# A mixture-of-experts stage in seven steps: every piece one step later, two sets of output banks, token buffers refilled after the combination, pads at the front of the buckets

## The reference, cut to what matters

```python
x = x + gnn(layernorm(x), adj, ...)               # two layers: softmax(h h^T) * adj, three projections, layernorm, relu
xt = layernorm(x).reshape(-1, 384)
route_prob = softmax((xt @ enc_w + enc_b) @ sw_w + sw_b)
expert = argmax(route_prob)                       # one of 8 for each token
h = gelu(xt @ w1[expert] + b1[expert])            # 384 -> 64
out = (h @ w2[expert] + b2[expert]) * max(route_prob)
x = x + out
```

## Time and profile before

| | |
|---|---|
| median of the runs | 2221.36 us |
| profiled execution | 2229.13 us |
| its span, first to last instruction | 2227.4 us |
| mean granted TensorE clock | 0.986 |
| TensorE (PE) busy | 95% |
| VectorE (DVE) busy | 75% |
| ScalarE (ACT) busy | 67% |
| GpSimd (POOL) busy | 63% |
| DMA queue of SP | 99.6 MB, 15.1% of 16 engines |
| DMA queue of GpSimd | 50.6 MB, 6.0% of 16 engines |

### The profile page before, as it was taken

One profiled execution on the slowest core, in us unless ns is written; L12 is line 12 of the kernel. 1 busy time (PEld: TensorE's weight loads), 2 busy tenths in 40 slices (PEclk: granted clock), 3 DMA queues, 4 the chain that ended last, 5 costly groups with the idle time before them and its releaser, 6 DMA issues. The chain is left out here.

```text
span 2227.4 us, 56587 instructions
## 1 busy us (share of the span) xinstructions
PE 2116.7 (95%) x13576; PEld 2035.7 (91%) x13577; DVE 1661.4 (75%) x5442; ACT 1496.4 (67%) x3901; POOL 1405.0 (63%) x3274
## 2 busy tenths in 40 slices
PE   6999999999999999999999999999999999578886
PEld 5999999999999999999999998999999999456665
DVE  4777777777777777777777776777777777657775
ACT  4777777677676776677777766776777766356664
POOL 2556666666666666666666666666666666535555
PEclk9999999999999999999999999999999999789998
DMA  7101111111111111111111111111111111256664
GB/s 188 31 26 49 49 37 49 49 45 49 41 45 49 49 45 50 42 49 49 49 43 47 49 49 42 45 49 49 46 48 41 45 49 33 105 184 208 221 224 144
DMA packets 94261, 153.77 MB, mean 69 GB/s; under 512 B 17627, under 2 KB 70700, under 8 KB 93954
## 3 DMA queue, kind: packets, MB, share of 16 engines
q1 hardware_dynamic: 75844, 99.61, 15.1%
q0 software_dynamic: 17408, 50.62, 6.0%
q10 hardware_dynamic: 704, 0.10, 0.0%
HBM read 96.11 MB, written 57.32 MB: 69 GB/s over the span
## 5 line engine op out<-in xcount | busy, mean ns | idle before, releaser
L421 PE MATMUL bank<-wT_hi,hT_hi 128*128 128x384 f32 x2304 | 797.9, 346 | 11.4 <-issue 5.4
L423 PE MATMUL bank<-wT_hi,hT_lo 128*128 128x384 f32 x2304 | 774.5, 336 | 0.0
L422 PE MATMUL bank<-wT_lo,hT_hi 128*128 128x384 f32 x2304 | 773.0, 336 | 0.0
L421 PEld LDWEIGHTS bank<-wT_hi,hT_hi 128*128 128x128 f32 x2304 | 434.9, 189 | 19.2 <-ACT bank L614 11.1
L422 PEld LDWEIGHTS bank<-wT_lo,hT_hi 128*128 128x128 f32 x2304 | 435.0, 189 | 0.0
L423 PEld LDWEIGHTS bank<-wT_hi,hT_lo 128*128 128x128 f32 x2304 | 433.8, 188 | 0.0
L1145 POOL TENSOR_TENSOR hT_lo<-hT,hT_hi 128x384 fp32r<-128x384 f32 x256 | 263.5, 1029 | 23.9 <-ACT hT_hi L679 22.4
L674 ACT ACTIVATE hT<-bank 128x384 f32<-128x384 f32 x256 | 126.1, 493 | 202.5 <-PE bank L413 180.9
L650 ACT CAST right_hi<-bank 128x384 fp32r<-128x384 f32 x256 | 123.0, 480 | 180.1 <-PE bank L423 179.2
L1548 POOL DMA_INDIRECT out_dram<-out_rows,tok x144 | 144.1, 1000 | 136.4 <-DVE out_rows L1519 100.7
L1200 POOL TENSOR_SCALAR_AFFINE_SELECT deltaT_hi<-turned_hi 128x128 fp32r<-128x128 f32 x256 | 87.7, 343 | 216.0 <-ACT turned_hi L656 208.5
(11 more groups left out here) (183 smaller groups left out, 5142.9 us busy)
## 6 DMA issues: line engine op xcount, KB each, us to landing
tok<-buckets SPq DMA_DIRECT2D x72, 388.0 KB
x_in<-in_x_dram SPq DMA_DIRECT2D x128, 192.0 KB, 2.5
x_res<-in_x_dram SPq DMA_DIRECT2D x128, 192.0 KB, 2.4
adj_in<-in_adj_dram SPq DMA_DIRECT2D x128, 64.0 KB, 2.4
buckets<-pads SPq DMA_DIRECT2D x9, 388.0 KB
out_dram<-out_rows,tok POOLq DMA_INDIRECT x144
buckets<-rows,dest_words POOLq DMA_INDIRECT x128, 2.8
w_top<-in_L_ffn_w_dram SPq DMA_DIRECT2D x2, 768.0 KB
```

Source lines behind the costliest of these rows:

```text
L421: pe.matmul(o, hi, w_hi, start=False, stop=False, skip_group_check=True)
L422: pe.matmul(o, hi, w_lo, start=False, stop=False, skip_group_check=True)
L423: last = pe.matmul(o, lo, w_hi, start=False, stop=(c == C - 1), skip_group_check=True)
```

## The change

1. **Pads at the front.** Every expert's rows now begin FRONT = 256 rows after e x CAP, and the pads fill the 256 rows ahead of them. Their place is known at compile time, and SP stores all nine pad tiles in step 26 of the graph stage (PAD_STEP = FIRST - 1). The last tile of an expert is no longer its rows and pads behind them: it is the last 256 rows before the expert's end, so that it repeats rows of the tile ahead of it, or takes in front pads.
2. **Tile table by partitions.** `tile_table` works on 72 partitions, one for each tile, with small operations; the number of tiles of an expert comes by rounding with 2^23 in place of a comparison with 64 limits. Two transposes on TensorE turn rows and experts back to one partition; a matmul and two more operations make `again`, a table that adds 32768 to the token number of every repeated row, so that the scatter leaves it out.
3. **Refill.** `load(j)` waits for `y_ready` of tile j-8 (combined) and for `ids_kept` in place of the landing of its scatter. The token numbers are therefore copied out of `tok`, with `again` added, by a new GpSimd operation `keep_ids` into `row_ids`, in step j+2, ahead of the scatters of tile j-4.
4. **Seven steps.** Copies in step j+2 (before j+1), `hidden` j+3 (j+2), gelu j+4 (j+2), `output` j+5 (j+4), `combine` and `store` j+6 (j+5). ScalarE does its gelu first in a step. `output` has two sets of two banks and waits for tile j-2; `hidden` moves into the free halves of the transposes' second banks, which adds one wait for gelu each to `turn` and `copy_last`.

The diff, cut to its core:

```diff
-    TILES_OF = TOKENS // TILE
+    FRONT, ROUNDER = TILE, float(1 << 23)
...
+                        if isinstance(i, int) and i == PAD_STEP:
+                            sp.wait_ge(pads_made, 1)
+                            for row in [e * CAP for e in range(E)] + [TAIL]:
+                                sp.dma_start(buckets[row:row + TILE, :].rearrange("(p t) w -> p t w", t=T), pads[:]
+                                             ).then_inc(pads_stored, 16)
...
                     steps(sp, first_steps)
-                    sp.wait_ge(pads_made, 1)
-                    sp.dma_start(buckets[TAIL:TAIL + TILE, :].rearrange("(p t) w -> p t w", t=T), pads[:]
-                                 ).then_inc(pads_stored, 16)
-                    sp.wait_ge(ends_ready, 1)
-                    for e in range(E):
-                        row = sp.value_load(end_words[0:1, e:e + 1], min_val=e * CAP, max_val=e * CAP + TOKENS)
-                        sp.dma_start(buckets[bass.ds(row, TILE), :].rearrange("(p t) w -> p t w", t=T), pads[:]
-                                     ).then_inc(pads_stored, 16)
...
+                    pe.wait_ge(table_done, 2)
+                    pe.transpose(rows_of, per_tile["row"][0:TILES, :], ident[0:TILES, 0:TILES])
+                    pe.transpose(experts_of, per_tile["expert_at_most"][0:TILES, :], ident[0:TILES, 0:TILES]
+                                 ).then_inc(table_turned, 1)
+                    pe.wait_ge(table_done, 3)
+                    pe.matmul(twice_of, per_tile["twice_wide"][0:TILES, :], ident[0:TILES, 0:TILES], start=True, stop=True
+                              ).then_inc(table_turned, 1)
...
                         dve.wait_ge(ends_done, 1)
-                        dve.tensor_copy(end_words[:], ends_of[0:1, :]).then_inc(ends_ready, 1)
                         dve.wait_ge(route_consts_made, 1)
-                        dve.tensor_tensor(o["held"][:], ends_of[0:1, :], o["bases"][:], ALU.subtract).then_inc(table, 1)
+                        dve.tensor_tensor(o["held"], ends_of[0:TILES, :], o["bases"], ALU.subtract).then_inc(table, 1)
...
-                        dve.tensor_tensor(o["filled_tiles"][:], o["starts"][:],
-                                          o["held"][:].unsqueeze(2).broadcast_to([1, E, TILES_OF]), ALU.is_lt
+                        dve.tensor_scalar(o["rough"], o["held"], 1.0 / TILE, (TILE - 1) / 2.0 / TILE, ALU.mult, ALU.add
-                        dve.tensor_reduce(o["tiles_of"][:], o["filled_tiles"][:], AX_X, ALU.add).then_inc(table, 1)
...
+                        dve.tensor_scalar(o["rounded"], o["rough"], ROUNDER, None, ALU.add).then_inc(table, 1)
+                        dve.wait_ge(table, 4)
+                        dve.tensor_scalar(o["tiles_of"], o["rounded"], ROUNDER, None, ALU.subtract).then_inc(table, 1)
+                        dve.tensor_tensor(o["lower_tiles"], o["lower"],
+                                          o["tiles_of"].unsqueeze(1).broadcast_to([TILES, E, E]), ALU.mult
+                        dve.tensor_reduce(o["tiles_upto"], o["lower_tiles"], AX_X, ALU.add).then_inc(table, 1)
+                        dve.tensor_scalar(o["behind"], o["tiles_upto"], o["number"][:, 0:1], None, ALU.is_le
...
-                        dve.tensor_tensor(o["behind"][:], o["numbers"][:],
-                                          o["tiles_upto"][:].unsqueeze(1).broadcast_to([1, TILES, E]), ALU.is_ge
-                        dve.tensor_reduce(o["expert"][:], o["behind"][:], AX_X, ALU.add).then_inc(table, 1)
-                        dve.tensor_tensor(o["skipped"][:], o["behind"][:],
-                                          o["skip"][:].unsqueeze(1).broadcast_to([1, TILES, E]), ALU.mult
+                        dve.tensor_reduce(o["expert"], o["behind"], AX_X, ALU.add).then_inc(table, 1)
+                        dve.tensor_tensor_reduce(o["skipped"], o["behind"], o["tiles_of"], 1.0, 0.0, ALU.mult, ALU.add,
+                                                 o["skip"]).then_inc(table, 1)
...
+                        dve.scalar_tensor_tensor(o["own_end"], o["experts"], o["expert"][:, 0:1], o["ends"],
+                                                 ALU.is_equal, ALU.mult).then_inc(table, 1)
+                        dve.scalar_tensor_tensor(o["in_expert"], o["skip"], -float(TILE), o["straight"],
+                                                 ALU.mult, ALU.add).then_inc(table, 1)
+                        dve.tensor_reduce(o["end"], o["own_end"], AX_X, ALU.add).then_inc(table, 1)
+                        dve.scalar_tensor_tensor(o["in_buckets"], o["expert"], float(CAP), o["in_expert"],
                                                  ALU.mult, ALU.add).then_inc(table, 1)
-                        dve.tensor_scalar(tile_row[:], o["row"][:], float(TAIL), None, ALU.min).then_inc(tiles_ready, 1)
+                        dve.tensor_scalar(o["row"], o["end"], -float(TILE), o["in_buckets"][:, 0:1], ALU.add, ALU.min
+                                          ).then_inc(table_done, 1)
+                        dve.wait_ge(table_done, 2)
+                        dve.tensor_tensor(o["twice"], o["in_buckets"], o["row"], ALU.subtract).then_inc(table, 1)
+                        dve.wait_ge(table_turned, 1)
+                        dve.tensor_copy(tile_row[:], rows_of).then_inc(tiles_ready, 1)
+                        dve.tensor_copy(tile_expert[:], experts_of).then_inc(tiles_ready, 1)
+                        dve.wait_ge(table, 15)
+                        dve.tensor_scalar(o["twice_wide"], ones[0:TILES, :], o["twice"][:, 0:1], None, ALU.mult
+                                          ).then_inc(table_done, 1)
+                        dve.wait_ge(table_turned, 2)
+                        for t in range(T):
+                            dve.tensor_scalar(again[:, :, t], twice_of, per_tile["position"][:, t:t + 1], float(2 * TOKENS),
+                                              ALU.is_gt, ALU.mult).then_inc(tiles_ready, 1)
...
-                            dve.memset(counts[1][:, BATCH, e:e + 1], float(e * (CAP // P))).then_inc(filled, 1)
+                            dve.memset(counts[1][:, BATCH, e:e + 1], float((e * CAP + FRONT) // P)).then_inc(filled, 1)
...
-            hidden_banks = (bank[4], bank[5])
-            y_banks = (bank[6], bank[7])
-
-            OUTPUT, GELUS, DEPTH = 4, 4, 5
+            FREE_HALF = slice(TILE, 2 * TILE)
+            hidden_banks = (bank[1][:, FREE_HALF], bank[3][:, FREE_HALF])
+            y_banks = ((bank[4], bank[5]), (bank[6], bank[7]))
+
+            COPIES, HIDDEN, GELU, OUTPUT, DEPTH = 2, 3, 4, 5, 6
+            GELUS = 4
...
                         if past(j, RING):
-                            sp.wait_ge(stored[k % OUT_RING], 16 * T // OUT_RING * (j - RING - k % OUT_RING) + 16 * T)
+                            sp.wait_ge(y_ready, T * (j - RING) + T)
+                            sp.nop(nofuse=True)
+                            sp.wait_ge(ids_kept, j - RING + 1)
                         row = sp.value_load(tile_row[0:1, j:j + 1] if isinstance(j, int) else
                                             tile_row[0:1, bass.ds(j, 1)], min_val=0, max_val=TAIL)
...
+                        if past(j, 4):
+                            pe.wait_ge(gelu_ready, j - 3)
...
-                        o = hidden_banks[k % 2][:, 0:TILE]
+                        o = hidden_banks[k % 2]
...
-                            if past(j, 1):
-                                pe.wait_ge(y_ready, T * (j - 1) + t + 1)
-                            o, rows = y_banks[t][:, 0:D], slice(t * P, (t + 1) * P)
+                            if past(j, 2):
+                                pe.wait_ge(y_ready, T * (j - 2) + t + 1)
+                            o, rows = y_banks[k % 2][t][:, 0:D], slice(t * P, (t + 1) * P)
...
                     def step(i, k):
                         if there(i - 1):
                             turn(i - 1, k - 1)
-                        if there(i - 2):
-                            hidden(i - 2, k - 2)
+                        if there(i - HIDDEN):
+                            hidden(i - HIDDEN, (k - HIDDEN) % RING)
                         if there(i - OUTPUT):
                             output(i - OUTPUT, (k - OUTPUT) % RING)
...
                     def step(i, k):
+                        if there(i - GELU):
+                            gelu(i - GELU, (k - GELU) % RING)
                         if there(i):
                             normalise(i, k)
-                        if there(i - 1):
-                            pick_w1(i - 1, k - 1)
-                            copy_first(i - 1, k - 1)
-                        if there(i - 2):
-                            gelu(i - 2, k - 2)
-
-                    act.wait_ge(tiles_ready, 1)
+                        if there(i - COPIES):
+                            copy_first(i - COPIES, (k - COPIES) % RING)
+                            pick_w1(i - COPIES, (k - COPIES) % RING)
...
@@ -1497,6 +1535,7 @@
```

(29 more changed lines are left out.)

81 lines of the change are left out of this document (43 added, 38 removed).

## The result

The changed kernel takes 2167.91 us at the median of four runs (2166.76 to 2170.39), the kernel before, beside it, 2221.69 (2217.87 to 2224.03): a ratio of 0.976, with a 95% interval from 0.9748 to 0.9772. 2186.1 us was predicted, in a range from 2156 to 2212. The gain is 54 us, not 35. The profiled execution took 2170.39 us, its span is 2168.4. (The profiled execution of before lay 7.8 us above its median; so the spans differ by 59.0 us, the medians by 54.)

A forecast was written before the change was run, and what follows sets the result against it. A ring of load latencies was taken to bound the expert stage. First scatter 1966.3, plus scatters 185.8, kept numbers 36.7 and landing 3.3 gave 2192.1, 35.3 under the old span; from 2221.4 that gives 2186.1 us, range 2156 to 2212.

The forecast's parts named there:

- rival A: Expert stage: GpSimd paces, at 3.0 to 3.25 us a tile, 2177 to 2195 us; chance 0.43.
- B: Expert stage: TensorE paces, kept numbers cost 0.2 us or less, 2.66 to 2.85 us a tile, 2153 to 2167 us; chance 0.20.
- the ring of loads: Expert stage before: buffer refill waits for scatters to land; a turn of 10.5 to 12.3 us sets 3.53 us a tile.
- Pads and table: Hand-over to the expert stage: pads moved to step 26 bring the first load 5.7 us earlier; the table costs nothing.
- The memsets: VectorE at the hand-over: 4.1 us long, would begin near 1945.4, end at 1949.5, just covered by the first loads.
- One more step at the start: Opening of the expert stage: the added step delays the first scatter by 2.66 us.
- The kept numbers: GpSimd in the expert stage: one small operation a tile, 0.54 us each, 68 counted, 36.7 us.
- rival F: GpSimd blocked by VectorE's normalisation and cast through the port: 3.88 us a tile, 2241 us; chance 0.03.
- The ring after: Expert stage after: refill turn of 5.3 us needs 2.1 us a step, 3.1 with slow landings; no longer decides.
- Two sets of banks and seven steps: Expert stage: removes TensorE's waits for the previous tile's combination, letting it come to 2.66 us a tile.
- C: Expert stage: transfers pace, landings grow by 2 to 3 us, 3.3 to 3.5 us a tile, 2199 to 2213 us; chance 0.25.
- D: Expert stage: another wait keeps 3.53 us a tile, only the hand-over's gain less the added step stays, 2218 us; chance 0.05.

The follow-up runs named there:

- the fourth group: Rerun on a chip of its own: the changed kernel with the old steps and one set of output banks; 2163.05 us, ratio 0.9727.
- the pause: Changed kernel with VectorE filling a spare tile in four writes in step 7, read by nobody; 2170.30 us, ratio 0.9772.
- the quickest kernel: Changed kernel with the old steps and one set of output banks, new refill kept, in its later run; 2163.05 us, ratio 0.9727.
- the third: Changed kernel unaltered 2166.66 us; with one set of output banks 2168.44; with spare VectorE writes 2170.30; with old steps and two sets 2171.99.
- the second group: Changed kernel with kept numbers done twice, 2216.89 us; without the lower half's product, 2210.95; with half-row loads, 2232.20; with kept numbers by ScalarE, 2222.91.

## Why the prediction was right, and where not

**The forecast as a whole.** The range held the result, but rival A did not: 2167.91 us lies outside its 2177 to 2195 and just above B's 2153 to 2167, and B's condition (kept numbers of 0.2 us or less) and pace (2.66 to 2.85 us a tile) are what came. That the range took in most of B made the forecast come out, more than the sum did.

**What bounded the kernel before** was read rightly: the ring of loads. With the refill behind the combination and the old steps, 60.8 us go; pads, table and kept numbers without that refill had brought 4.4, in another group. Two details of the working were wrong. The landing of 2.65 us that it puts into the turn ends at 2068.51 + 2.65 = 2071.16, behind the refill at 2070.30, so it belongs to the next buffer, and the 12.3 us made with it has no row behind it. And the normalisation starts 0.25 us behind the combination of its step (median of 40 tiles), not 1.1. With the median turn of those tiles, 10.9 us, three steps cover 3.55 us each, so the ring still gives today's pace.

**Pads and table.** First load at 1947.2 forecast, 1947.79 measured. The pads were priced at 11.6 us of SP's time, took 8.3, and cost nothing, as said. The table ends at 1943.0, within its 1944.8. The memsets were late next, as named: they begin at 1946.61, where 1945.4 was forecast.

**One more step at the start** was priced at 2.66 us, and this was wrong. From the first load to the first scatter it is 16.6 us, before it was 16.4, and with the old steps in the fourth group 16.5. My reading, which no run tests, is that the opening is paced by its loads and by hand-overs within a step, and that the seven steps shorten the second as they add a step. First scatter: 1966.3 forecast, 1964.37 measured.

**GpSimd as the bound** is right in part. In the changed kernel its idle time is its least gaps and 1.3 us more in 150, the last combination ends at 2157.1 and the last scatter starts 7.0 us behind it, and the last combinations themselves wait for scatters (timeline of the changed kernel's end):

```profile
2153.82 1.14 DVE L1558 SCALAR_TENSOR_TENSOR out_rows<-bank,tok 128x384 f32<-128x384 f32 x2 [0.76 <-DMA out_dram<-out_rows,row_ids]
...
2155.98 1.14 DVE L1558 SCALAR_TENSOR_TENSOR out_rows<-bank,tok 128x384 f32<-128x384 f32 x2 [1.01 <-DMA out_dram<-out_rows,row_ids]
```

No experiment moved GpSimd's load and had no late signals, so this stands on the trace of four kernels (the changed one, the one with one set of banks, the one with the pause, the quickest) and not on an edit. And what feeds GpSimd is hardly quicker. Over the 40 tiles from the 17th to the 57th of the changed kernel the combinations come 2.75 us apart and their scatters 2.78; a scatter starts 1.0 us behind the end of its combination at the start of these tiles and 2.2 at their end. So two bounds lie within 0.03 us a tile, and a quicker GpSimd alone would have gained little. The second bound can be TensorE, which is busy 49.21 of 50 us (50.00 in the quickest kernel, where the combinations come 2.68 us apart and the scatters 2.71), or the ring of loads (below); no run separates them. Rival B is thus nearly as true as A.

**The kept numbers** are the term that was mis-sized: 0.54 us forecast, 0.10 in the rows above. The busy time was right, 0.20 us against a median of 213 ns (min/median/max ns, changed kernel, 1985 to 2140 us):

```profile
L1588 POOL TENSOR_TENSOR row_ids<-tok,again x55: 209/213/603, 1986.4 to 2137.7; 128x2 int32<-128x2 int32 x55
```

Both gaps were wrong. I took 0.18 ahead of it and a gap of 0.46 in place of 0.30 behind it, from rows where GpSimd had waited or followed a chain of its own. Where its inputs are long there and a scatter precedes, there is 0.01 to 0.02 ahead and 0.16 behind, less than the gap between two scatters. I had named that for rival B ("part of the 0.30 may overlap") and weighed it low. In the sum, 185.8 + 36.7 = 222.5 us were forecast from the first scatter on; it is 199.8 + 0.98. These 21.7 us and the 1.9 of the first scatter are the difference of 2192.1 and 2168.4. The kept numbers alone, at 0.10 us, take 68 x 0.44 = 29.9 off, so that some 8 us came on elsewhere and hid a part of the error: slower scatters, and the idle time of the opening and the end.

**Scatters** were taken at 2.58 us a tile. They are slower beside a full VectorE: 1033 ns on the mean, at most 1225. The rule of the Trainium skill that the prediction weighed ("SBUF — State Buffer", section "Who interferes with whom") names copies, casts and tensor_scalars, and for these the changed kernel does not bear it out on scatters. 39 of 144 scatters take over 1.05 us, and 38 of these lie beside the split L1549, a subtraction with both inputs in SBUF. The 70 scatters beside that split take 1.07 us on the mean, the 74 others 0.99, most of them beside a copy, a cast or a tensor_scalar. One of the slow ones:

```profile
2040.20 0.42 DVE L1549 TENSOR_TENSOR gelu_bottom<-gelu_out,gelu_top 64x256 fp32r<-64x256 f32 x1
...
2040.35 1.13 POOL L1598 DMA_INDIRECT out_dram<-out_rows,row_ids  x1 [0.16 <-issue]
```

Of the 14 kept numbers over 0.30 us, 11 (0.30 to 0.60) lie beside the normalisation, a tensor_scalar, where 24 lie in all; on them the rule may show, but small. In the quickest kernel as many scatters, 69, lie beside the split, but only 13 of all are over 1.05 us, and those beside it take 1.01 us on the mean, the others 1.00; so lying beside it is not enough. Some 0.1 us a tile comes of it, 2 x (1.033 - 0.98), where rival F had 0.76. Why the other order of steps is spared most of it stays open.

**The ring after** was put at 2.1 us a step, 3.1 with slow landings. The page of the changed kernel gives the median landing in its last column:

```profile
tok<-buckets SPq DMA_DIRECT2D x72, 388.0 KB, 4.5
```

So a turn is about 1.1 + 1.0 + 4.5 = 6.6 us, and two steps must cover that less 1.1: 2.75 us each. That is what the combinations do, 2.75 us apart, against 2.80 of the scatters: the ring is at its limit, as ScalarE's wait of 30.7 us for loads says, and just short of deciding the total. The median turn of 40 tiles, 6.7 us, and a normalisation 1.2 us behind its combination give the same. With the old steps the ring has three steps and ScalarE waits 3.2 us between 1980 and 2110 us, at a quicker pace:

```profile
ACT n_rows L1479 <- DMA tok<-buckets: 3.2, 8, 0.6
```

**Two sets of banks and seven steps** were credited with TensorE's waits. They bring nothing that the runs can show: with one set the median is 1.8 us higher, inside the intervals, and the kernel without either is no slower, 0.9727 against 0.9756 and 0.976. I had said that seven steps leave the ring two steps, and did not ask what the old steps with the new refill would give, which was at least as good a kernel.

**Rivals.** C's mechanism, landings that grow, was there (4.5 us, where 3.1 were taken) and put the ring of loads level with GpSimd; its pace of 3.3 to 3.5 was not. D, E and F did not come.

**Open.** What makes TensorE's signals late. The same program took 2223.99 and 2163.05 us on two chips, so it isn't the program alone; whether it is the chip or the hour, and whether the changed kernel too is hit there, was not seen, as it never ran in those groups. The medians of the kernel before differ by 6.7 us between the groups with late signals and the third; that it loses so little because its ring leaves the room is argued, not tested. The change by halves was also never run in one group without late signals: the old refill with seven steps stands on a group that had them. For the four kernels of the second group nothing follows as to what paces; whether the kept numbers by ScalarE gain something is open.

## What to carry to other kernels

A chain of latencies that runs through a ring is best cut at its earliest safe release, and that cut should be tried alone before steps are added, since each step more between load and release takes one from what the ring covers. An engine is at its limit where none of its waits exceeds its least gap, and the pace of what feeds it says how much a quicker one would bring; the longest entry in the list of waits may belong to an engine with room. An experiment without the kernel under study in its own group can mistake the chip for the edit.

## What the runs showed of the hardware

- TensorE's signals can reach the others up to some 2.7 us after the end that the trace gives its matmul (2063.47 to 2066.16), time and again, on two of the chips, while single instructions of SP take 0.7 us instead of 0.02. The refill alone took 61 us of 2224 more (2.7%) on the chip where its trace shows this than on one where it doesn't.
- A small operation of GpSimd ahead of an indirect DMA costs 0.10 us net where its inputs are there: 0.02 ahead of it, its 0.22, and 0.16 instead of 0.30 behind it.
- The DMA engines kept a share of 0.90 at 284 GB/s over 50 us with landings of 4.5 us at the median; where the share was 0.67, the prediction read one of 3.1.
